# One instruction for both channel halves in layer 2's scan loop, and the state sum of the second half in a TensorE accumulator

## What is computed

```python
def step(h, inp):                       # over the tokens; h: [batch, 256, 16]
    dt_t, B_t, C_t, x_t = inp
    h = jnp.exp(dt_t[..., None] * A) * h + dt_t[..., None] * B_t[:, None, :] * x_t[..., None]
    y = jnp.einsum('ben,bn->be', h, C_t)
    return (h, y)
...
y = (y + x_main * D_param) * jax.nn.silu(z)
y = jnp.einsum('ble,de->bld', y, W_out)
...
h = jax.nn.silu(jnp.einsum('nd,edh->enh', xt, we1) + be1[:, None, :])
eo = jnp.einsum('enh,ehd->end', h, we2) + be2[:, None, :]
y = xt + jnp.einsum('ne,end->nd', w, eo)
```

## Time and profile before

| | |
|---|---|
| median of 3 runs | 1637.55 us (1633.42 to 1638.33) |
| the profiled execution | 1637.49 us, its span 1635.7 us, mean granted TensorE clock 0.885 |
| Vector busy | 1070.3 us, 65% of the span |
| TensorE busy | 1261.6 us, 77% of the span |
| ScalarE busy | 724.0 us, 44% of the span |
| GpSimd busy | 599.8 us, 37% of the span |

### The profile page before, as it was taken

The page is one execution under the profiler, slowest core; times in us unless marked ns, Lnnn a source line. Parts: engine busy times, 40 slices in busy tenths (PEclk is TensorE's granted clock), DMA queues, the critical chain, the costliest instruction groups (busy, mean ns, idle before and its releaser), DMA issues. The chain is left out here.

```text
span 1635.7 us, 21776 instructions
## 1 busy us (share of the span) xinstructions
PE 1261.6 (77%) x7188; PEld 859.3 (53%) x7188; DVE 1070.3 (65%) x2581; ACT 724.0 (44%) x1526; POOL 599.8 (37%) x597
## 2 busy tenths in 40 slices
PE   1799999998997764666768865976784885888985
PEld 0345564554554653544564652653553554666664
DVE  1266767678786353565556995995997798634444
ACT  0255545544544243333236745653671672343322
POOL 1243344443348533332201441442343244225551
PEclk9999999999999787777787997898797798799998
DMA  8200000000000122430000000000000000001113
GB/s 172 80 1 1 1 1 1 1 1 1 1 6 28 52 78 58 129 116 7 8 1 1 1 0 1 1 0 0 1 0 1 1 1 1 27 14 34 35 34 90
DMA packets 54315, 40.36 MB, mean 25 GB/s; under 512 B 13175, under 2 KB 46685, under 8 KB 54205
## 3 DMA queue, kind: packets, MB, share of 16 engines
q1 hardware_dynamic: 35516, 23.91, 5.0%
q0 software_dynamic: 4544, 9.32, 2.1%
q10 hardware_dynamic: 14146, 5.75, 1.7%
HBM read 25.92 MB, written 13.04 MB: 24 GB/s over the span
## 5 line engine op out<-in xcount | busy, mean ns | idle before, releaser
L762 POOL TENSOR_TENSOR PR<-PR,R 128x256 f32<-128x256 f32 (+3 forms) x128 | 160.9, 1258 | 270.8 <-DVE R L1216 266.0
L1637 POOL TENSOR_TENSOR SA<-SA,H 128x512 f32<-128x512 f32 x64 | 81.6, 1275 | 258.4 <-DVE H L1864 258.4
L1859 DVE TENSOR_TENSOR_SCAN H<-DAS,H 128x512 f32<-128x512 f32 x128 | 174.2, 1399 | 0.0
L415 PEld LDWEIGHTS banks<-we,HH 128*128 128x128 f32 x1024 | 147.3, 214 | 10.3
L415 PE MATMUL banks<-BCR,identR 96*128 96x512 f32 x256 | 110.9, 520 | 53.9 <-DVE H L1864 44.3
L1033 ACT ACTIVATE PR<-banks,NM 128x129 f32<-128x129 f32 (+3 forms) x256 | 132.5, 526 | 43.7 <-DVE NM L1193 42.8
L415 PE MATMUL banks<-we,HH 128*128 128x128 f32 x1024 | 146.4, 297 | 0.0
L415 PEld LDWEIGHTS banks<-PTS,V 128*64 128x64 f32 x1280 | 73.0, 144 | 99.1 <-issue 90.6
L415 PE MATMUL banks<-XNT,we 128*128 128x512 f32 x256 | 120.7, 594 | 0.0
L415 PE MATMUL banks<-PTS,V 128*64 128x128 f32 x1280 | 105.4, 296 | 16.3 <-DVE PTS L1201 9.4
L1201 DVE COPY PTS<-banks 128x128 f32<-128x128 f32 (+3 forms) x128 | 62.2, 486 | 80.9 <-PE banks L903 78.5
(11 more groups left out here) (516 smaller groups left out, 2665.3 us busy)
## 6 DMA issues: line engine op xcount, KB each, us to landing
xsort<-zrow SPq DMA_DIRECT2D x1, 3072.0 KB, 13.1
XS<-xsort SPq DMA_DIRECT2D x12, 256.0 KB, 2.9
ysort<-PTS SPq DMA_DIRECT2D x12, 256.0 KB, 2.2
pj_stage<-in_L_ffn_w_proj SPq DMA_DIRECT2D x1, 2048.0 KB, 9.9
we<-in_L_ffn_we SPq DMA_DIRECT2D x1, 2048.0 KB, 9.6
we<-yrows SPq DMA_DIRECT2D x8, 256.0 KB, 5.0
X<-in_L_attn_resid_pre ACTq DMA_DIRECT2D x4, 256.0 KB, 4.6
xrows<-XN SPq DMA_DIRECT2D x4, 256.0 KB, 2.3
```

The lines of the kernel that those rows point to most:

```text
L415: return nc.tensor.matmul(o, l, r, start=start, stop=stop)
L762: nc.gpsimd.tensor_tensor(p, p, R[:, n, :].unsqueeze(2).to_broadcast([P, 2, w]), ALU.mult).then_inc(pn, 1)
L1637: nc.gpsimd.tensor_tensor(Y[m], Y[m], H[:, n % 2, m, :], ALU.add).then_inc(ya, 1)
L1859: nc.vector.tensor_tensor_scan(H[:, n % 2, m, :], DA[:, n % 4, m, :], H[:, n % 2, m, :], 0.0, ALU.mult, ALU.add).then_inc(scn, 1)
```

## The change

Vector's three instructions of a state each take both halves at once, as 128x1024: the inputs product and the C product read the same row twice, and the scan runs over both halves laid end to end. For that the decay of the second half's first token is set to zero by a memset of `DA[:, :, 1, 0:1]` ahead of the loop, and ScalarE writes that half's decays from its second token on. Vector's order becomes scan(n), inputs(n + 1), C product(n). `H` gets a third slot. GpSimd adds the first half alone, into its own tile `YY`. The second half is summed over the states by TensorE: `sum_half(n)` multiplies the identity with `H` and accumulates in bank 5, and Vector adds that bank to `YY` once at the end. The ring of hidden goes from four banks to three. GpSimd's initial product with `Dp` and Vector's multiplication with the gate take both halves at once as well. TensorE's list stays in its order, with `sum_half(n)` behind C row n + 1.

```diff
@@ -1591,7 +1591,7 @@
             dtp, dta, dte, dtl, dtx = (lsem(f"a2_{k}") for k in ("dt_raw", "dt_abs", "dt_exp", "dt_log", "dt_x"))
             bp, cp = lsem("a2_b_rows"), lsem("a2_c_rows")
             bm, ex, scn, hc, ya = (lsem(f"a2_{k}") for k in ("inputs", "decays", "scans", "outs", "y"))
-            yg, wo = lsem("a2_gated"), lsem("a2_projected")
+            yg, wo, yc = lsem("a2_gated"), lsem("a2_projected"), lsem("a2_half_summed")
             r = {k: lsem(f"f2_{k}") for k in ("logits", "shifted", "expd", "weights", "wT", "wT_stored", "bias")}
             r1, r1s, hp, hs, yp, ad, gt = (lsem(f"f2_{k}") for k in (
                 "router", "router_stored", "hidden", "silus", "outs", "added", "gate"))
@@ -1603,7 +1603,8 @@
                 DT = sbr("DT", [P, 2, S], c=c)
                 DTX = sbr("DTX", [P, 2, S], c=c)
                 DAS = sbr("DAS", [P, 8 * S + 4], c=c)
-                H = sbr("H", [P, 2, 2, S], c=c)
+                H = sbr("H", [P, 3, 2, S], c=c)
+                YY = sbr("YY", [P, 2, S], c=c)
                 BCR = sbr("BCR", [96, 2, S], F32R, c=c)
                 ACC = sbr("ACC2", [P, T, D], c=c)
                 H1 = sbr("H1", [P, S], c=c)
@@ -1614,7 +1615,7 @@
                 XP = DAS[:, 6 * S:8 * S + 4].rearrange("p (m s) -> p m s", m=2)
                 DBC = DAS[0:96, 4 * S:5 * S]
                 E, LN = DA[:, 0, :, :], DA[:, 1, :, :]
-                Y = [SA[:, :, :].rearrange(flat), H1[:, :]]
+                Y = YY[:, :, :]
                 GS = H1[:, :].rearrange("p (t d) -> p t d", t=T)
                 GG = DT[:, 0, :].rearrange("p (t d) -> p t d", t=T)
                 GB = DT[:, 1, :].rearrange("p (t d) -> p t d", t=T)
@@ -1626,15 +1627,13 @@
                         g.wait_ge(var, 1)
                         norm_pool(plink, mv[:, :, 1], rstd[:, :]).then_inc(rs, 1)
                         g.wait_ge(r["logits"], 1)
-                        for m in range(2):
-                            g.wait_ge(xs, m + 1)
-                            nc.gpsimd.tensor_tensor(Y[m], XM[:, m, :], Dp[:, m:m + 1].to_broadcast([P, S]),
-                                                    ALU.mult).then_inc(ya, 1)
+                        g.wait_ge(xs, 2)
+                        nc.gpsimd.tensor_tensor(Y, XM[:, :, :], Dp[:, :].unsqueeze(2).to_broadcast([P, 2, S]),
+                                                ALU.mult).then_inc(ya, 1)
                         for n in range(NS):
-                            for m in range(2):
-                                g.wait_ge(hc, 2 * n + m + 1)
-                                g.wait_ge(ya, 2 * n + m + 1)
-                                nc.gpsimd.tensor_tensor(Y[m], Y[m], H[:, n % 2, m, :], ALU.add).then_inc(ya, 1)
+                            g.wait_ge(hc, n + 1)
+                            g.wait_ge(ya, n + 1)
+                            nc.gpsimd.tensor_tensor(Y[:, 0, :], Y[:, 0, :], H[:, n % 3, 0, :], ALU.add).then_inc(ya, 1)
                         g.wait_ge(gt, 1)
                         nc.gpsimd.tensor_tensor(GG, GS, gamma[:, :].unsqueeze(1).to_broadcast([P, T, D]),
                                                 ALU.mult).then_inc(gt, 1)
@@ -1652,11 +1651,11 @@
 
                         def hidden(n):
                             e, k = divmod(n, 4)
-                            if n >= 4:
-                                pe.wait_ge(hs, n - 3)
+                            if n >= 3:
+                                pe.wait_ge(hs, n - 2)
                             elif n < 2:
                                 pe.wait_ge(zg, n + 1)
-                            mm(PS[:, 2 + n % 4, :], we1[:, e, k * P:(k + 1) * P], XNT[:, :]).then_inc(hp, 1)
+                            mm(PS[:, 2 + n % 3, :], we1[:, e, k * P:(k + 1) * P], XNT[:, :]).then_inc(hp, 1)
 
                         def outs(n):
                             u, t = divmod(n, 4)
@@ -1676,6 +1675,10 @@
                                 last = mm(PS[:, k, :], identR[0:96, i:i + 1].to_broadcast([96, P]), BCR[:, part, :],
                                           start=part == 0, stop=part == 1)
                             last.then_inc(done, 1)
+
+                        def sum_half(n):
+                            pe.wait_ge(hc, n + 1)
+                            mm(PS[:, 5, :], ident[:, :], H[:, n % 3, 1, :], start=n == 0, stop=n == NS - 1).then_inc(yc, 1)
 
                         for n in range(3):
                             hidden(n)
@@ -1708,14 +1711,15 @@
                                 if n % 2:
                                     work += [(hidden, 2 * n - 2 + 4 * LEAD + k) for k in range(4)]
                             if n + 1 < NS:
-                                pe.wait_ge(bm, 2 * n + 2)
+                                pe.wait_ge(bm, n + 1)
                                 rows(n + 1, 0, bp)
                             half = len(work) // 2
                             for f, i in work[:half]:
                                 f(i)
                             if n + 1 < NS:
-                                pe.wait_ge(hc, 2 * n + 2)
+                                pe.wait_ge(hc, n + 1)
                                 rows(n + 1, 1, cp)
+                            sum_half(n)
                             for f, i in work[half:]:
                                 f(i)
                         pe.wait_ge(yg, 1)
@@ -1744,7 +1748,7 @@
                             act.wait_ge(hp, n + 1)
                             if e >= 2 and k == 0:
                                 act.wait_ge(yp, e - 1)
-                            nc.scalar.activation(HH[:, e % 2, k, :], PS[:, 2 + n % 4, :], ACT.Silu,
+                            nc.scalar.activation(HH[:, e % 2, k, :], PS[:, 2 + n % 3, :], ACT.Silu,
                                                  bias=be1f[:, e, k:k + 1]).then_inc(hs, 1)
 
                         hidden(0)
@@ -1772,12 +1776,12 @@
 
                         def decays(n):
                             if n >= 4:
-                                act.wait_ge(scn, 2 * (n - 3))
+                                act.wait_ge(scn, n - 3)
                             elif n == 2:
                                 act.wait_ge(dtp, 2)
                                 act.wait_ge(bcr, 1)
                             for m in range(2):
-                                nc.scalar.activation(DA[:, n % 4, m, :], DT[:, m, :], ACT.Exp,
+                                nc.scalar.activation(DA[:, n % 4, m, m:], DT[:, m, m:], ACT.Exp,
                                                      scale=Aneg[:, m, n:n + 1]).then_inc(ex, 1)
                         act.wait_ge(dtx, 1)
                         decays(0)
@@ -1825,7 +1829,9 @@
                         v.wait_ge(dta, 2)
                         link(nc.vector.tensor_tensor(DT[:, :, :], DT[:, :, :], DTX[:, :, :], ALU.add))
                         v.wait_ge(dtl, 1)
-                        nc.vector.tensor_tensor(DT[:, :, :], DT[:, :, :], LN, ALU.add).then_inc(dtx, 1)
+                        link(nc.vector.tensor_tensor(DT[:, :, :], DT[:, :, :], LN, ALU.add))
+                        v.wait_ge(dtp, 2)
+                        nc.vector.memset(DA[:, :, 1, 0:1], 0.0).then_inc(dtx, 1)
                         v.wait_ge(r["wT"], 1)
                         nc.vector.tensor_copy(WGT[0:NE, :], PS[0:NE, 6, :]).then_inc(r["wT_stored"], 1)
                         v.wait_ge(dtx, 1)
@@ -1847,28 +1853,38 @@
                             last.then_inc(ad, 1)
 
                         v.wait_ge(dtx, 2)
+
+                        def row_of(k):
+                            return PS[:, k, :].unsqueeze(1).to_broadcast([P, 2, S])
+
+                        def inputs(n):
+                            v.wait_ge(bp, n + 1)
+                            if n >= 3:
+                                v.wait_ge(ya, n - 1)
+                                v.wait_ge(yc, n - 2)
+                            nc.vector.tensor_tensor(H[:, n % 3, :, :], DTX[:, :, :], row_of(0), ALU.mult).then_inc(bm, 1)
+
+                        def scan(n):
+                            h = H[:, n % 3, :, :].rearrange("p m s -> p (m s)")
+                            v.wait_ge(bm, n + 1)
+                            v.wait_ge(ex, 2 * n + 2)
+                            nc.vector.tensor_tensor_scan(h, DA[:, n % 4, :, :].rearrange("p m s -> p (m s)"), h, 0.0,
+                                                         ALU.mult, ALU.add).then_inc(scn, 1)
+
+                        inputs(0)
                         for n in range(NS):
-                            v.wait_ge(bp, n + 1)
-                            for m in range(2):
-                                if n >= 2:
-                                    v.wait_ge(ya, 2 * n + m - 1)
-                                nc.vector.tensor_tensor(H[:, n % 2, m, :], DTX[:, m, :], PS[:, 0, :], ALU.mult).then_inc(bm, 1)
-                            for m in range(2):
-                                v.wait_ge(bm, 2 * n + m + 1)
```

(20 more changed lines are left out.)

## The result

The changed kernel takes 1681.35 us (median of 4 runs, 1676.48 to 1682.62), against 1636.7 for the kernel before on the same chip: a ratio of 1.027 [1.0244, 1.0296]. 1681 was forecast. The profiled execution took 1676.48 us, 39.0 more than the one of before; it is the shortest of the four, 4.9 under their median.

The account below looks back on a forecast made before the run. Vector was taken to set the pace, TensorE close behind; after the change their circle of waits would. 1637.5 + 42.4 for four stages + 0.8 outside the loop = 1681 us, 80 in 100, own range 1668 to 1697.

Parts of the forecast that it names:

- The order decides: Layer-2 loop: TensorE issues B row n+1 behind the previous step's tail, with one scan as cover; inputs(n+1) stalls 1.3 or 0.9 us.
- The circle: C product to next inputs product, 4.73 or 3.04 us, plus 2.33 to the C product's end: 12.43 a pair, 1.40 more.
- The stage: One layer-2 loop, inputs(0) to the gate's end: plus 2.5, 7.6 and 0.5, so 10.6 us; four stages 42.4.
- the five pairs: Steady stretch from inputs(3) to inputs(13): 54.51 us before, 5 x 12.43 = 62.15 after, plus 7.6 a stage.
- the end: Stretch from inputs(13) to the end of the gate: 19.57 us before, 20.1 after, plus 0.5 a stage.
- Vector's merges: Three merges for each of 64 states on Vector, about 0.06 us each: 12 us saved if Vector stays the bound.
- GpSimd: One add per state: scan goes first and unharmed on even n, loses 0.26 on odd; contention shrinks from 0.76 a pair.
- The sum: sum_half on TensorE is two instructions like hidden: 0.86 us a state, 1.72 a pair.
- The rival of one pass: sum_half takes one pass: 0.43 us less on some 13 steps a stage, 22 us, giving 1659; 5 in 100.
- The rival that TensorE stays at its lower level longer: Lower clock for two more steps a stage, about 2.5 us each: 20 us, giving 1701; 8 in 100.
- The ring of three banks: Hidden's banks on TensorE: no cost, as 3.1 us of work and a Vector stall cover the wait for SiLU.
- The range's own terms: Merges saving nothing add 8 us, GpSimd first on even n adds 10, a start at the high level takes off 10.

## Why the prediction was right, point by point

- **The order decides.** Right, in mechanism and size. The circle was put at 4.73 and 3.04 from a C product to the inputs product, measured 4.72 and 3.04; stalls of 1.3 and 0.9, measured 1.21 and 0.83; a pair 12.43, measured 12.46 (62.32 / 5, below). One row moved on TensorE, or one product moved on Vector, takes the loss away.
- **The stage.** inputs(0) to inputs(3) was put at 18.4, measured 18.24; the five pairs at 62.15, measured 62.32; the end at 20.1, measured 20.46. The last was put too low because the last C product reads the scan right ahead of it (2.38 from start to start, not 2.18) and the final add waits 0.46, not 0.3. A stage grew by 10.97 us in place of 10.6, the four by 44.2 in place of 42.4. That the median lands on 1681 to the microsecond is in part luck: the profiled execution grew by only 39.0 us, mostly since its first loop begins 4.4 us earlier, and the other three took 4.8 to 6.1 us longer than it; no trace shows where.
- **Vector's merges.** The products follow each other after 1.13, as put; the scan after 2.21, between the 2.18 taken and the upper end of 2.25. Where the order is right, they and the lighter GpSimd give a pair of 10.20. The pair and the merged product, 1.27 and 1.21 long, bear out the rows' 0.06. The fixed cost of each instruction in the Trainium skill (VectorE: DVE Perf Modes, section on the TRN2 errata) would have made the merges worth 30 us, an estimate; the trace does not agree with it.
- **GpSimd.** Right: on even n the scan starts first (915.38), takes 2.29 and holds the add (915.54) for 3.19; on odd n the scan takes 2.55, 0.27 more, where 0.26 was put.
- **The sum.** Two passes: 909.01 to 909.88 is 0.87, 0.86 forecast. The rival of one pass falls.
- **The clock.** The rival that TensorE stays at its lower level longer falls. Counted from inputs(0) of the first stage, the granted clock is 0.50 for 10.8 us (882.41 to 893.20), before for 11.0 (886.84 to 897.86); the windows at 890 us differ, 0.84 against 0.61, because the loop starts 4.4 us earlier. Behind C product 1, which ends at 895.93, inputs(3) already starts after 4.72 us, the odd step's time at the high level.
- **Small terms.** The memset takes 0.06 us, not 0.2. The ring of three banks costs nothing, as put: the hidden layers take 120.7 us and TensorE idles 0.0 ahead of them, as in the earlier trace rows. The loss sits in the wait named beforehand, with 16.8 us a stage (67.0 / 4) where "some 14" stood; that sum left out the long waits at the start, 3.20 and 2.51. The range's own terms (up by 8 and 10, down by 10) give 1671 to 1699, not the 1668 to 1697 that the prediction states; the result lies in both.

## What to carry to other kernels

When an instruction is moved up on one engine, look at where its producer stands in the list of the other: in an engine that works in order, a producer that stands behind a wait for the consumer's own result makes a circle, and any work put into that circle lengthens each turn (46.7 us in all for the sum here, against 13.6 with the row ahead of the wait). If neither engine is full in the window and each waits for the other, reorder before you remove work. And look behind the loop too: when work moves from one engine to another, the loop's end and what follows it can change.

## What the runs showed of the hardware

- Two 512-wide products in a row take 1.27 us, one lone 0.69, one 1024-wide 1.21: the start of an instruction hides under the one before, unless it reads that one's result; with Vector's old order that cost 0.11 (a scan behind the product) and 0.19 (a product behind the scan).
- A scan over 1024 columns takes 2.28 us. A GpSimd add of 1.27 that starts 0.16 after it takes 3.19 and leaves it unharmed; one that started 0.87 ahead of it costs it 0.27.
- The same 16 projections took 2.05 us at a granted clock of 1.00 after TensorE had idled 1.42 us, and 3.32 after 2.51 idle, at a mean of 0.58 over the projections themselves. Idle time right ahead of them does not settle it alone: in the kernel before they took 2.05 at 1.00 behind 3.44 and 3.54 us idle (second and third stage), and 3.39 at 0.58 behind 5.06 (first). An edit inside a loop can so change the time of matmuls behind it that it doesn't touch.
